# Softmax sums of an attention kernel: one row of sums broadcast after the reciprocal, or sums made on all 128 partitions before it

## What is computed

```python
q = (x @ wq.T + bq).reshape(B, T, H, D)          # k, v alike; a rotation per head
scores = jnp.einsum('btkgd,bskd->bkgts', qg, k) * scale
mask = jnp.tril(jnp.ones((T, T)))
scores = scores + mask                            # added, not a cut: every key counts
p = jax.nn.softmax(scores, axis=-1)
out = jnp.einsum('bkgts,bskd->btkgd', p, v).reshape(B, T, C)
return out @ wo.T + bo
```

## Time and profile before

| what | us |
|---|---|
| median of 5 runs | 8925.7 |
| the five runs | 8925.7, 8589.38, 8946.74, 8941.07, 8595.15 |
| the profiled execution | 8593.42 |
| its span, first to last instruction (core 3, the slowest) | 8591.9 |
| spans of the 8 cores | 8548.8 to 8591.9 |
| busy in the span: TensorE matmuls, VectorE, ScalarE | 4824.1, 2893.6, 2104.4 |

### The profile page before, as it was taken

How to read it: one execution, slowest core, us unless ns; L and a number is a source line. 1 busy time by engine, 2 the same in 40 slices (tenths; PEclk the granted TensorE clock), 3 DMA queues, 4 the chain that set the end, 5 groups by cost and what they waited for, 6 DMA issues and landing times.

```text
span 8591.9 us, 68750 instructions; the slowest of 8 cores (8548.8 to 8591.9 us)
## 1 busy us (share of the span) xinstructions
PE 4824.1 (56%) x20170; PEld 1969.4 (23%) x20170; DVE 2893.6 (34%) x3673; ACT 2104.4 (24%) x2102; POOL 357.4 (4%) x659
## 2 busy tenths in 40 slices
PE   5645556655554555666652545555456665644736
PEld 2211112211221121222221222222222232222312
DVE  0034454445444545444444122222111113122031
ACT  0033444444433444444422011111000001011011
POOL 0000000000000000000000000000111110000000
PEclk9867777777777787888886668888788887877868
DMA  7741111111122111000012222222222222334233
GB/s 94 91 92 56 58 55 57 55 63 51 58 93 88 57 54 57 18 5 6 3 71 75 56 91 99 96 99 100 92 85 89 85 79 93 113 112 143 94 110 110
DMA packets 393377, 645.24 MB, mean 75 GB/s; under 512 B 210613, under 2 KB 304822, under 8 KB 370999
## 3 DMA queue, kind: packets, MB, share of 16 engines
q1 hardware_dynamic: 277128, 356.11, 13.3%
q0 software_dynamic: 67824, 227.06, 9.8%
q10 hardware_dynamic: 48064, 57.68, 2.1%
HBM read 484.01 MB, written 197.13 MB: 79 GB/s over the span
## 4 chain that ended last, share of the span: by engine, by line
PE 37%; DVE 26%; ACT 14%; DMA 12%; issue 7%; SPq 2%; DVEq 1%; POOL 1%; ACTq 0%; another core or an unknown queue 0%; POOLq 0%
ACT arena L156 8%; DVE arena L156 8%; PE pH L156 8%; DVE stat L156 7%; PE pG L156 7%; PE pA L156 5%; PE pC L156 4%; PE pE L156 4%; DVE y L156 3%; PE pB L156 3%; PE pD L156 3%; PE pV L156 2%; ACT i32q L156 2%; DMA w2f<-w 2%; PE pT L156 2%
## 5 line engine op out<-in xcount | busy, mean ns | idle before, releaser
L156 PE MATMUL pV<-arena,v_tm 128*128 128x512 bf16 x2048 | 734.6, 446 | 792.3 <-ACT arena L156 481.2
L156 DVE TENSOR_TENSOR arena<-arena 128x1024 bf16<-128x1024 bf16 x992 | 686.6, 692 | 1147.7 <-ACT arena L156 1033.9
L156 ACT ACTIVATE arena<-pA,beta_s 128x1024 bf16<-128x1024 f32 x512 | 571.0, 1115 | 684.2 <-PE pA L156 531.5
L156 ACT ACTIVATE arena<-pB,beta_s 128x1024 bf16<-128x1024 f32 x512 | 571.0, 1115 | 645.3 <-PE pB L156 284.5
L156 PE MATMUL pT<-consts,xqrow 128*128 128x128 bf16 x1408 | 125.2, 241 | 1073.1 <-DVE w1t L156 572.7
L156 PE MATMUL pG<-w1t,xq_fm 128*128 128x512 bf16 x2816 | 643.5, 388 | 78.2 <-DVE htile L156 51.2
L156 PE MATMUL pH<-w1t,xq_fm 128*128 128x512 bf16 x2816 | 666.5, 398 | 0.0
L156 PE MATMUL pA<-arena,k_fm 128*128 128x512 bf16 x1024 | 470.1, 459 | 3.5 <-DVE x2t L156 3.5
L156 PEld LDWEIGHTS pV<-arena,v_tm 128*128 128x128 bf16 x2048 | 168.8, 105 | 1274.5 <-issue 1258.5
L156 PE MATMUL pB<-arena,k_fm 128*128 128x512 bf16 x1024 | 453.8, 443 | 0.1
L156 PE MATMUL pD<-w2full,hq_fm 128*128 128x512 bf16 x1408 | 344.7, 406 | 127.2 <-DMA w2full<-w2qT_d 127.2
(11 more groups left out here) (119 smaller groups left out, 5493.8 us busy)
## 6 DMA issues: line engine op xcount, KB each, us to landing
w1f<-w SPq DMA_DIRECT2D x88, 1024.0 KB, 5.5
w2full<-w2qT_d SPq DMA_DIRECT2D x64, 1408.0 KB, 13.6
w1q_d<-w1qb POOLq DMA_DIRECT2D x176, 256.0 KB, 2.8
h_d<-htile POOLq DMA_DIRECT2D x176, 256.0 KB, 2.3
w2f<-w ACTq DMA_DIRECT2D x16, 2816.0 KB, 12.2
hrow<-h_d SPq DMA_DIRECT2D x16, 2816.0 KB, 9.7
xqrow<-w1q_d SPq DMA_DIRECT2D x72, 512.0 KB, 3.3
w2q_d<-w2qb POOLq DMA_DIRECT2D x16, 1408.0 KB, 12.9
```

The costliest lines, as they stand in the source:

```text
L156: ins = getattr(e, meth)(*args, **kw)
```

## The change

- A constant ones_b is added: ones in 128 x 128, bf16, with its input, its place behind ONESF in consts (ONESB) and one more load on SP's queue.
- At the end of a head the sums are made with ONESB instead of ONESC, so that all 128 partitions of pA hold the same sums. The reciprocal reads pA on 128 partitions and writes recipb whole, in float32. The cast to recrob, the broadcast pair into pB and the copy from pB are gone. ve_recb is now the same count as ve_recip: scores of both j = 0 and j = 1 wait for the reciprocal.
- In the q chain the matmul for the squared norms also uses ONESB and writes all of pC; only row 0 is read, as before. It waits for ve_sgc[0] too. The operations on the row and the broadcast by onesrb stay.

```diff
-        consts = sb(es, "consts", [128, H * D + 257], BF16)
+        consts = sb(es, "consts", [128, H * D + 385], BF16)
+        ONESB = consts[:, H * D + 257:H * D + 385]
...
+        P.op("sync", "dma_start", out=ONESB, in_=onesb_d, inc=(ldi, 16))
...
                 nsm = P.op("tensor", "matmul",
-                           pC[0:1, th * 512:th * 512 + 512], ONESC,
+                           pC[:, th * 512:th * 512 + 512], ONESB,
                            qpre[:, th * 512:th * 512 + 512],
                            start=True, stop=True,
-                           waits=[(ac, nsq)] if th == 0 else (), inc=(pe, 1))
+                           waits=[(ac, nsq), (ve, ve_sgc[0])]
+                           if th == 0 else (), inc=(pe, 1))
...
                     n_sums = P.op("tensor", "matmul",
-                                  pA[0:1, th * 512:th * 512 + 512], ONESC,
+                                  pA[:, th * 512:th * 512 + 512], ONESB,
                                   root_ap[:, th * 512:th * 512 + 512],
                                   start=True, stop=True,
                                   waits=[root_rdy, (ac, exp_slot2[0])]
                                   if th == 0 else (), inc=(pe, 1))
-                P.op("vector", "reciprocal", recro, pA[0:1, 0:TG],
-                     waits=[(pe, n_sums)], inc=(ve, 1))
-                recrob = attn[0:1, h * TG:h * TG + TG]
-                ve_recip = P.op("vector", "tensor_copy", recrob, recro,
+                ve_recip = P.op("vector", "reciprocal", recipb[:],
+                                pA[:, 0:TG], waits=[(pe, n_sums)],
                                 inc=(ve, 1))
-                n_rb = 0
-                for th in range(TH):
-                    n_rb = P.op("tensor", "matmul",
-                                pB[:, th * 512:th * 512 + 512], onesrb[:],
-                                recrob[0:1, th * 512:th * 512 + 512],
-                                start=True, stop=True,
-                                waits=[(ve, ve_recip), (ac, exp_slot2[1])]
-                                if th == 0 else (), inc=(pe, 1))
-                ve_recb = P.op("vector", "tensor_copy", recipb[:],
-                               pB[:, 0:TG], waits=[(pe, n_rb)], inc=(ve, 1))
+                ve_recb = ve_recip
                 at_cnt = P.op("vector", "tensor_tensor",
                               attn[:, h * TG:(h + 1) * TG], pV[:, 0:TG],
                               recipb[:], ALU.mult,
-                              waits=[(pe, npv_last), (ve, ve_recb)],
+                              waits=[(pe, npv_last), (ve, ve_recip)],
                               inc=(ve, 1))
```

More of the change, by code:

```diff
@@ L67, in host_consts @@
                 .astype(BF),
+                ones_b=np.ones((128, 128), dtype=np.float32).astype(BF),
                 scale_col=np.full((128, 1), D ** -0.25, dtype=np.float32))
@@ L242, in _build @@
     onesf_d = dt("ones_f", [128, 128], BF16, kind="ExternalInput").ap()
+    onesb_d = dt("ones_b", [128, 128], BF16, kind="ExternalInput").ap()
     scalec_d = dt("scale_col", [128, 1], F32, kind="ExternalInput").ap()
@@ L1539, in make_in_maps @@
         ones_rowb=consts["ones_rowb"], ones_f=consts["ones_f"],
-        scale_col=consts["scale_col"])
+        ones_b=consts["ones_b"], scale_col=consts["scale_col"])
     in_maps = []
```

## The result

| | before | changed |
|---|---|---|
| median of all executions | 8673.7 us (10) | 8703.0 us (6) |
| lowest | 8589.4 us | 8525.6 us |
| changed over before | | 0.9922, 95% interval 0.9904 to 0.994 |

The changed kernel took 8525.6, 8527.6 and 8532.2 us, the one before 8589.4 to 8598.5. So 0.8% went, or 67 us of about 8595. That is within 2%, as forecast, and somewhat more than the 51 us of the sum.

The account below looks back on a forecast made before the run. Bound by a chain across engines, notably 32 seams between attention heads. First group 26.9, second 19.4, last heads 7.0, weight loads -1.9: 51.4 us off 8593.4 gives 8542.0 us; range 8500 to 8580.

Parts of the forecast that it names:

- the 51 us of the sum: Whole kernel: 51.4 us saved by both groups' seams and the two last heads, less the weight loads.
- Cast and pair in the chain, copy beside it: Inner seam: cast and broadcast matmuls delay the scores, the copy does not; removing them saves 1.79 us.
- The wide reciprocal: Seam: 128 partitions instead of one add 12 ns or 1% (0.07 us) each; taken as nothing.
- The weight load: Sums and q chain: loading the square of ones costs 0.03 us more in 64 uses, 1.9 us if exposed.
- The wait on ve_sgc and the extra load: q chain and kernel start: the wait costs nothing; the extra constant load nothing, at worst 0.4 us.
- The ends of the groups: Last head of each group: every removed link counts, so the load of wo comes 3.51 us sooner, twice.
- Rivals 3 and 4: Seam: 3, slower wide reciprocal, 8752 at twice the time, chance 0.05; 4, scores held by something else, 8588, chance 0.03.
- a shift passes through whole: First group, masked blocks behind the seam: the full 1.79 us reaches the head's end, 15 times, 26.9 us.
- I expect the same mixture: First group: seven of fifteen inner seams with an early third exp, eight with one 0.76 us later, as before.
- left is 1.29 us: Second-group seams: the clock takes back 0.5 of 1.79 us because more work runs at half speed; 15 times, 19.4 us.
- Rival 1: Seams and start of second-group heads: the clock takes most back, leaving 17 us, 8576; gains under 40 us, chance 0.17.
- the 8874: Forecast time in us with the same saving for an execution of the upper group, whose median was 8925.7.

Follow-up runs that it names:

- q_only: Kernel before with only ones_b, its load and the q chain's part of the change; lowest 8602.4 us, before beside it 8595.6.
- warm_q: Changed kernel plus three unread matmuls into pC behind each of blocks 12 to 17, ahead of the q projection; lowest 8586.7 us, before beside it 8607.6.
- pad_cast_2: Changed kernel with one 1x1024 row cast put back behind the wide reciprocal, profiled a second time; lowest 8600.2 us, before beside it 8611.7.

## Why the prediction was right and wrong

**Right, by its own steps.** Cast and pair in the chain, copy beside it: the first exp came 1.84 us sooner (1.79; the scores wait 0.14 us and not 0.24, and the four take 1.88 and not 1.83). The wide reciprocal: 12 ns, the lower of the two bounds. The Trainium skill (VectorE: DVE Perf Modes, "Why tensor_reduce can't reduce along partition axis") calls the lanes independent pipelines, and the 12 ns agree with that. The weight load: 26 ns more (0.03 us), and in q_only nothing of it reaches the heads. The wait on ve_sgc and the extra load: nothing that shows. The ends of the groups: 3.45 us (3.51). Rivals 3 and 4 are out by the reciprocal's 6558 ns and by the 0.14 us in front of the scores.

**Wrong: what becomes of the seam's gain in the rest of the head.** The steps that failed are "a shift passes through whole", with "I expect the same mixture", for the first group (15 x 1.79 = 26.9 us) and "left is 1.29 us" for the second (19.4). On core 4 they were 53.4 and 12.0; over the cores read 15 x 3.1 = 47 and 15 x 1.1 = 17. The second comes near only as a mean of unlike heads: the first five of the group gained 1.5 us each, the late ones 0.8, the last one 2.5.
- *Second group.* I looked for the clock's part only in the 10 us behind the seam. There the term held in the mean, the third exp of a late head stands 1.4 us sooner, but not the step that gives it. At the late seams of before the clock rose 4.4 to 5.5 us after TensorE's first work (6.4 at two of 72); in the changed kernel it rose after 5.1 to 6.0 us at 28 of 36 and after 2.6 or 2.7 at the others, and the third exp is 1.2 or 2.2 us sooner. The next head's q projection, 45 us later, lay outside my view. In 28 of 36 late heads it meets a low stretch and takes 1.6 us more; the rest of the head is 0.5 shorter, and 0.25 of the seam's 1.84 are left. The two kinds of heads in one trace show where it goes. warm_q shows that without the low stretch such a head is 0.8 us shorter, not the full 1.7. That it is the earlier start that makes the projection meet it is read from the traces and not shown by a run of its own.
- *First group.* The mixture of seams did not stay. The third exp was late (by 0.76 us) at about 0.6 of the inner seams of before and at 0.2 of the changed kernel's, which is 0.3 us of the surplus of 1.3. About 0.3 us each lie just ahead of the projection, at the projection (9.4 to 9.1 us in the mean, with the granted clock there from 0.92 to 0.95) and around the 27th exp, and the last head alone became 5.5 us shorter. pad_cast_2 shows by experiment that the group answers to 0.79 us at the seam with 1.7 us per head. That the clock does this is read from the traces; no experiment took these places alone, and why the first group gains more than the seam stays open.
- I treated the head's length as a sum of links that stay as they are. Equal lengths (92.2 us with first exps at 10.66, 9.59 and 9.41; 88.7 and 88.8 with 7.99 and 4.65) come out of unlike parts, as the second table shows, so a saving can count for little or for more than itself. Rival 1 named the mechanism, but put it at the seam and at 17 us in all. (Its rise "about 3.9 us later" should read 9.4 - 5.3 = 4.1 by its own rows, which changes nothing.)

The sum fell 16 us short (51 us against 67): the first group's term was 20 us too small and the second's 2 to 7 too large, and start and end scatter by 10 us to either side. **The range** of 8500 to 8580 was drawn around the profiled execution alone and holds 8525.6 to 8532.2. The median of all executions, 8703.0, lies outside, and so does the 8874 that the text itself gave for executions like three of its five times: that is a fault of the range, not of the mechanism.

## What to carry to other kernels

Read a seam link by link and count only what stands in the chain; that was good to 0.05 us here. Then ask which long runs of matmuls downstream may meet another level of TensorE's clock once they start sooner, and look at the granted clock over each of them in several repetitions of the loop: if it differs between repetitions, a saving of one or two microseconds can be swallowed or doubled. Where TensorE idles while another engine works, a few matmuls that nobody reads can pay; here 16 of them gave about 27 us on top of the change (0.9922 to 0.9891 of 8600, intervals that overlap), and 12 with the scores freed from the reciprocal some 50 (71 by the ratios 0.9922 and 0.984, 53 by the lowest executions of one set). The same 16 in the kernel before gave nothing in its second group.

## What the runs showed of the hardware

- The reciprocal takes 6546 ns for 1 x 1024 and 6558 for 128 x 1024: the 127 further partitions cost 12 ns.
- After an idle time of 5.34 us TensorE's granted clock was 0.50 at its next matmuls; after one of 2.54 us the PV pair ran at the high level (0.59 us against 1.01), and the pair 1.3 us later at the low one (1.04). The Trainium skill (TensorE: Matmul & The Clock Gate, "What's actually happening") says that the low rate is the default and activity lifts it. The runs agree: matmuls without any use lifted it for the scores behind them.
- A low stretch inside the 32 matmuls of the q projection made them last 10.6 us instead of 8.9 (granted 0.84 and 1.00 in the mean). Removing it gave back 0.8 us of the 1.7, since the rest of the head grew by 0.9.
- Late heads came out equally long with unlike seams, 92.2 us in three kernels and 88.7 to 88.8 in two. I had not expected it. The parts show where each gain went; whether the head's length is drawn to these values is open.
